# Graph attention over an 8192 x 8192 matrix: half of the matrix's pieces issued from ScalarE's queue

## What is computed

```python
h = jnp.maximum(_layernorm(x, axis=-1), 0.0)
proj = jnp.einsum('nf,hfo->hno', h, W)
s_src = jnp.einsum('hno,ho->hn', proj, a_src)
s_tgt = jnp.einsum('hno,ho->hn', proj, a_tgt)
scores = jax.nn.leaky_relu(s_src[:, :, None] + s_tgt[:, None, :], negative_slope=0.2)
attn = jax.nn.softmax(adj[None, :, :] + scores, axis=1)      # down each column
vals = jnp.einsum('hij,hjo->hio', attn, proj) + h[None, :, :]
return x + jax.nn.elu(vals).mean(axis=0)
```

## Time and profile before

| | us |
|---|---|
| median of 3 runs | 993.73 |
| lowest and highest | 992.29, 1092.76 |
| the profiled execution | 993.13 |
| its span in the profile | 991.4 |

### The profile page before, as it was taken

The page is one execution under the profiler, slowest core; times in us unless marked ns, Lnnn a source line. Parts: engine busy times, 40 slices in busy tenths (PEclk is TensorE's granted clock), DMA queues, the critical chain, the costliest instruction groups (busy, mean ns, idle before and its releaser), DMA issues.

```text
span 991.4 us, 14968 instructions
## 1 busy us (share of the span) xinstructions
PE 734.1 (74%) x4995; PEld 609.6 (61%) x4995; DVE 807.4 (81%) x812; ACT 684.3 (69%) x1173; POOL 234.7 (24%) x164
## 2 busy tenths in 40 slices
PE   0419597797797797797797797797797798609882
PEld 0317477777777677677677677687687686504330
DVE  3976888888888888888888888888888877327996
ACT  0598496696696696696786786786786788544542
POOL 1000211221221221221212212212212202215885
PEclk9759798898898898898898898998998999859997
DMA  9999999999999999999999999999999976076111
GB/s 245 337 382 384 372 370 337 370 331 325 369 330 323 370 328 325 369 327 323 372 325 321 373 324 325 373 326 324 375 323 324 364 234 173 9 207 150 53 54 55
DMA packets 224068, 294.93 MB, mean 297 GB/s; under 512 B 4512, under 2 KB 218016, under 8 KB 224032
## 3 DMA queue, kind: packets, MB, share of 16 engines
q1 hardware_dynamic: 214816, 290.27, 85.7%
q0 software_dynamic: 9216, 4.20, 3.5%
HBM read 281.80 MB, written 12.65 MB: 297 GB/s over the span
## 4 chain that ended last, share of the span: by engine, by line
PE 33%; DVE 28%; issue 11%; ACT 10%; DMA 8%; POOL 6%; SPq 2%; ACTq 0%; POOLq 0%; DVEq 0%
PE ps L440 23%; DVE arena L561 19%; ACT ps L498 9%; PE ps L405 7%; DMA arena<-in_adj 6%; POOL arena L391 4%; DVE arena L570 3%; SPq L332 2%; DVE arena L578 2%; POOL arena L395 2%; DMA sums<-arena 2%; PE ps L424 1%; DVE arena L623 1%; ACT arena L519 1%; PE ps L412 1%
## 5 line engine op out<-in xcount | busy, mean ns | idle before, releaser
L498 ACT ACTIVATE ps<-ps,arena 128x1024 f32<-128x1024 f32 x512 | 556.0, 1086 | 225.6 <-PE ps L440 198.8
L440 PE MATMUL ps<-ident,arena 128*128 128x128 f32 x4096 | 572.3, 289 | 52.1 <-ACT ps L498 50.1
L440 PEld LDWEIGHTS ps<-ident,arena 128*128 128x128 f32 x4096 | 480.1, 149 | 130.3 <-ACT ps L498 126.3
L561 DVE TENSOR_TENSOR arena<-arena 128x3072 f32<-128x3072 f32 (+2 forms) x115 | 359.3, 3125 | 13.6 <-DMA arena<-in_adj 10.3
L378 POOL DMA_INDIRECT sums<-arena x64 | 157.0, 2453 | 641.4 <-DVE arena L617 313.6
L405 PE MATMUL ps<-ident,arena 128*128 128x128 f32 x512 | 93.2, 342 | 152.6 <-DVE arena L570 151.1
L405 PEld LDWEIGHTS ps<-ident,arena 128*128 128x128 f32 x512 | 80.7, 183 | 157.9 <-issue 89.0
L578 DVE TENSOR_REDUCE arena<-ps 128x1 f32<-128x1024 f32 x64 | 78.3, 1224 | 54.2 <-PE ps L405 54.2
L498 ACT ACTIVATION_READ_ACCUMULATOR ps<-ps,arena 128x1 f32 x512 | 100.2, 196 | 0.0
L557 DVE TENSOR_TENSOR arena<-arena 128x3072 f32<-128x3072 f32 (+2 forms) x23 | 71.8, 3122 | 16.4 <-DMA arena<-in_adj 16.4
L583 DVE SCALAR_TENSOR_TENSOR ps<-ps,arena 128x1024 f32<-128x1024 f32 x64 | 82.1, 1283 | 0.3 <-issue 0.3
(11 more groups left out here) (74 smaller groups left out, 195.8 us busy)
## 6 DMA issues: line engine op xcount, KB each, us to landing
arena<-in_adj SPq DMA_DIRECT2D x160, 1536.0 KB, 13.7
arena<-in_adj SPq DMA_DIRECT2D x16, 512.0 KB, 7.2
arena<-in_adj SPq DMA_DIRECT2D x8, 1024.0 KB, 11.0
sums<-arena SPq DMA_DIRECT2D x1, 4160.0 KB, 22.4
arena<-sums SPq DMA_DIRECT2D x8, 512.0 KB, 7.3
out<-arena SPq DMA_DIRECT2D x16, 256.0 KB, 2.3
sums<-arena POOLq DMA_INDIRECT x64, 7.2
w_sb<-in_L_gnn_W SPq DMA_DIRECT2D x1, 256.0 KB, 2.7
```

The costliest lines, as they stand in the source:

```text
L440: mm = pe.transpose(turned_ps[n % 2][:, m, :], piece(i, r, nq)[:, m, q * P:(q + 1) * P], ident[:, :])
L498: act.activation(turned_ps[n % 2], turned_ps[n % 2], ACT.Exp, scale=KAPPA, bias=cert[:, i, q, G:G + 1], accum_out=cert[:, i, q, r:r + 1]). ...
L561: dve.tensor_tensor(acc_of(nq), acc_of(nq), piece(i, r, nq), ALU.max).then_inc(f_acc, 1)
```

## The change

The pieces with odd r are no longer issued by SP, except those of the first 12 pieces. ScalarE issues them, in its own stream, right behind the exponential of the last chunk of the piece that held the slot (in strips of three sets, behind chunks 7, 11, 17 and 23). The exponential has waited for the turned chunk already, so no new wait is needed. Behind pieces 1 and 3 it is pieces 5 and 7 of the next strip, behind pieces 5 and 7 it is pieces 1 and 3 of the strip after that. SP still issues the even pieces, the loads of `x` and everything else, with the waits it had.

```diff
+    def issued_by_scalar(g, i, r):
+        return r % 2 == 1 and not (known(g) and number(g, i) * G + r < RING)
+
+    def load_piece(engine, g, i, r):
+        nq = subs(g, i)
+        cols = bass.ds(sets_to(g, i) * P, nq * P)
+        engine.dma_start(piece(i, r, nq), adj_r[r, :, :, cols]).then_inc(f_in[slot(i, r)], 16)
...
             def strip(g, i):
-                nq, Q = subs(g, i), number(g, i)
+                Q = number(g, i)
                 for r in range(G):
+                    if issued_by_scalar(g, i, r):
+                        continue
                     if not (known(g) and Q * G + r < RING):
                         sp.wait_ge(f_turn, turned_before(g, i, r))
...
-                    cols = bass.ds(sets_to(g, i) * P, nq * P)
-                    sp.dma_start(piece(i, r, nq), adj_r[r, :, :, cols]).then_inc(f_in[slot(i, r)], 16)
+                    load_piece(sp, g, i, r)
...
                     act.activation(turned_ps[n % 2], turned_ps[n % 2], ACT.Exp, scale=KAPPA, bias=cert[:, i, q, G:G + 1],
                                    accum_out=cert[:, i, q, r:r + 1]).then_inc(f_exp, 1)
+                    if q == nq - 1:
+                        into = latter_of(g, i) if r < AHEAD else latter_of(*latter_of(g, i))
+                        new = (r + AHEAD) % G if r < AHEAD else r - AHEAD
+                        if issued_by_scalar(*into, new) and not (known(into[0]) and number(*into) >= STRIPS):
+                            load_piece(act, *into, new)
```

## The result

| | before | after |
|---|---|---|
| median, us | 993.68 (4 runs) | 1001.52 (4 runs) |
| lowest to highest | 992.29 to 1092.76 | 1000.48 to 1003.19 |
| span of the profiled execution | 991.4 | 999.5 |

The ratio of after to before is 1.0085, with a 95% interval from 1.0065 to 1.0105: slower by 0.85%. One of the four runs of before, 1092.76, is far off the others; the ratio leaves it out.

What follows compares the result with a forecast made beforehand. Steady strips were taken as bound by a ring through VectorE's passes and ScalarE's exponentials and copy, the start by full DMA. 993.13 + 7.4 (start) + 0 = 1000.5, with the median 0.6 higher 1001; range 991 to 1031.

Steps and rivals of the forecast that it cites:

- The start, +7.4 us: Strips 0 to 2: four early ScalarE pieces delay strip 1's own pieces, making strip 2's last pass 7.4 us late.
- Sharing by halves: DMA engines: two queues with work each get half of the service, so the early pieces take their half.
- Case A: Rival, start: the early pieces do no harm; 993.7 us, between 991 and 997; chance 0.14.
- The issue hides on ScalarE, cost 0: Steady strips, behind chunks 7 and 11: each issue of 0.65 us fits under the running exponential of 1.10 us.
- Case B: Rival, chunks 7 and 11: issues not hidden, 1.3 us in each of 20 strips; 1027 us; chance 0.18.
- Piece 7 three us early: Steady strips: sharing lands piece 7 at about 486, 1.4 us later but still 3 us early; cost 0.
- the 4.4 us of slack: Steady strips, kernel before: piece 7 lands at 484.8, 4.4 us before the last pass wants it at 489.19.
- case C: Rival, steady strips: piece 7 comes too late or interleaved streams move less; up to +80 us, 1041; chance 0.08.
- Steady strips as before: Strip 3 on: strips stay at 37.5 us and VectorE's wait for the copy at 1.67 us; cost 0.
- ScalarE held in strip 0: Start, upper bound 11 us: a full queue holds ScalarE's four issues, bringing strip 1's first exponential some 4 us later.

Runs made afterwards that it cites:

- e2: Changed kernel, but ScalarE issues only pieces 5 and 7 of strip 1 and 1 and 3 of strip 2: 999.41 us, ratio 1.0063 to before.
- e3: Changed kernel, but ScalarE issues only pieces 1 and 3 of strip 2: 993.95 us, ratio 1.0001 to before.
- e4: Changed kernel, but ScalarE issues only pieces 5 and 7 of strip 1: 993.67 us, ratio 0.9999 to before.
- h1: Kernel before, with the clearing of sums cut in two and issued before piece 4 of strips 3 and 4: 986.17 us, ratio 0.9931.
- e1: Changed kernel, but ScalarE issues only the odd pieces of strips 3 and later: 1002.18 us, ratio 1.0084 to before.
- f5: f1 with each odd piece issued as two transfers of half the size: 992.15 us, ratio 1.0003 to before.
- f6: f1, but ScalarE issues pieces 1, 2, 5 and 6 and SP 0, 3, 4 and 7: 991.62 us, ratio 1.0001 to before.
- f1: Changed kernel, but ScalarE issues only the odd pieces of strips 6 and later: 993.97 us, ratio 1.0015 to before.
- f7: f1, but ScalarE issues all pieces from strip 6 on, SP none: 992.01 us, ratio 1.0002 to before.

## Why the prediction was right, point by point

1001 was forecast, in 991 to 1031, within 2% at 0.71; 1001.52 was measured. The forecast called 2% what a measurement of this kernel can tell from no change. The runs tell more: the interval is 0.4% wide, and the loss of 0.85% is clear of zero.

- **The start, +7.4 us.** Right in each step, and 0.7 short in size (8.1 at strip 3): last pass of strip 1 at 84.8 (85.02), strip 2 ready at 99.45 (99.53), its last pass at 122.3 (122.85), strip 3's first near 136.5 (137.20). e2 shows that the four early pieces make 7.0 us of it, e3 and e4 that it takes both of their effects, h1 that less work ahead of strip 2 gains time. Not foreseen was that the four pieces are sufficient but not the only way: without them (e1) two later issues, pieces 1 and 3 of strip 3, made strip 2 as late. The forecast took the four pieces for the place; the mechanism, a second queue going past a first that is in arrears, is wider.
- **Sharing by halves.** Right for the start (4.47 and 4.46 MB in 24 us). The page DMA: Bandwidth & Descriptors of the Trainium skill, section Queues, rings and completion order, says that a DMA engine takes the queues that have work in turn, packet by packet; that row agrees. Case A, no harm, falls.
- **The issue hides on ScalarE, cost 0.** Right: 0.56 us, inside the exponential, copy wait 28.4 us as before. Case B falls. In f5 the edge of the cover lies between 0.94 us of issuing, which hid, and 1.26, which held the next exponential by 0.35.
- **Piece 7 three us early.** Wrong. The step assumed that ScalarE's piece 5 gets its half of the bandwidth 2.2 us after its issue. It started only when piece 4 was nearly through, so 5 ran beside 6, and 7 beside the next strip's 0: 17.1 us to land and not about 14. All of the 4.4 us of slack went, and case C, given 0.08, was met at its edge: 8.7 us of waits in 17 strips. f6 shows the pairing as the cause. The term was booked at 0, and that it came out near 0 in spite of this was luck: the next point says what kept it there.
- **Steady strips as before.** Nearly right, 0.07 us each, but for a reason that was not in the working: most of the waits for piece 7 were given back by waits for TensorE that were 7.3 us shorter. f1 puts the steady part at 0.15% (0.05 to 0.26).
- **ScalarE held in strip 0.** Taken as the upper bound, 11 us. It was held 4.49 and 8.43 us, yet idled 13.52 us afterwards, so it added nothing.

## What to carry to other kernels

The second queue added no bandwidth here (384 GB/s between 46 and 90 us, before and after); it changed the order in which transfers are served, and where the first queue was in arrears the transfers on the second one went past those that waited, needed or not. Before giving part of a stream to another engine, list what waits in line at each of its issues and when each piece is wanted, the first strips above all. An issue of 0.55 us cost ScalarE nothing under a 1.1 us instruction; two of them, or one held by a fuller queue, outlasted it. The work to take out of a crowded start is what nobody waits for yet, such as the clearing here. And where work moves from one queue to another in the middle of a program, look at the strip of the switch by itself: in f7 it hid what the later strips gained.

## What was not expected of the hardware

- A transfer issued on the second queue 1.5 us behind one on the first got 3 packets in the 3.6 us from 476.4 on, while the first got 855; from 481 on both queues ran at 54.1% and 52.5% of the engines' time. Whether something ahead of the DMA engines keeps that order was not tried.
- Added waits of 7.1, 8.7 and 7.3 us for pieces and for the copy changed the time by only 0.15%, 0.03% and 0.02% in f1, f5 and f7, while the granted clock rose from 0.91 to 0.92, 0.93 and 0.97 and the waits for TensorE shrank by 7.1, 9.0 and 12.2 us. In f7 this was more than the added waits: its 14 strips were 3.6 us shorter, which the switch of queues in strip 5 took back.
